# Transformer block on one core: three banks each for scores and transposed scores, products of two steps and key sums in one group

## The reference, cut to what matters

```python
x = x + attn(layernorm(x))
x = x + ffn(layernorm(x))

def attn(x):                                  # H = 8, D = 16
    q = (x @ Wq.T).reshape(b, t, 2 * H, D)    # 16 heads of queries and keys
    k = (x @ Wk.T).reshape(b, t, 2 * H, D)
    v = (x @ Wv.T).reshape(b, t, H, 2 * D)    # 8 heads of values
    q, k = rope(q), rope(k)
    probs = softmax(einsum('bhtd,bhsd->bhts', q * D ** -0.5, k))
    diff = probs[:, :, 0] - lam * probs[:, :, 1]
    attn = einsum('bhts,bhsd->bhtd', diff, v)
    attn = attn * rsqrt(mean(attn * attn, -1) + 1e-5) * (1 - LAMBDA_INIT)
    return attn.reshape(b, t, e) @ Wo.T

def ffn(x):                                   # a gated cell over the 16 sequences, in order
    c = sigmoid(x_t @ wf.T + c @ uf.T + bf) * c + sigmoid(..wi, ui, bi) * tanh(..wc, uc, bc)
    return tanh(x @ wo.T + c_final @ uo.T + bo)
```

## Time and profile before

| | |
|---|---|
| median of 3 runs | 5261.81 us (5261.59 to 5262.73) |
| profiled execution | 5259.74 us, its span 5257.9 us |
| TensorE busy (PE) | 4979.5 us, 95% |
| VectorE (DVE) | 4021.4 us, 76% |
| GpSimd (POOL) | 2891.7 us, 55% |
| ScalarE (ACT) | 2722.8 us, 52% |

### The profile page before, as it was taken

One profiled execution on the slowest core, in us unless ns is written; L12 is line 12 of the kernel. 1 busy time (PEld: TensorE's weight loads), 2 busy tenths in 40 slices (PEclk: granted clock), 3 DMA queues, 4 the chain that ended last, 5 costly groups with the idle time before them and its releaser, 6 DMA issues.

```text
span 5257.9 us, 65030 instructions
## 1 busy us (share of the span) xinstructions
PE 4979.5 (95%) x24784; PEld 1695.8 (32%) x24784; DVE 4021.4 (76%) x6183; ACT 2722.8 (52%) x3173; POOL 2891.7 (55%) x2118
## 2 busy tenths in 40 slices
PE   6999999999999999999999999999999999999999
PEld 2224232332423223242332423233242322323237
DVE  6877777877778877777887777787777887777526
ACT  1464645556465554545556454554546555463652
POOL 3573746647275573727657374664727557372750
PEclk7899999999999999999999999999999999999999
DMA  6031221302222131222303122130222213122117
GB/s 141 26 60 46 50 64 37 69 37 58 52 45 69 33 64 40 45 66 51 67 26 62 45 45 69 34 72 37 54 56 45 69 33 61 43 45 59 65 49 280
DMA packets 127706, 311.05 MB, mean 59 GB/s; under 512 B 27297, under 2 KB 30498, under 8 KB 113442
## 3 DMA queue, kind: packets, MB, share of 16 engines
q1 hardware_dynamic: 124178, 289.33, 23.2%
q10 hardware_dynamic: 3216, 17.57, 0.9%
HBM read 172.07 MB, written 99.61 MB: 52 GB/s over the span
## 4 chain that ended last, share of the span: by engine, by line
PE 64%; DVE 16%; issue 13%; POOL 3%; ACT 3%; DMA 0%; ACTq 0%; POOLq 0%; SPq 0%; DVEq 0%
PE o_ps L792 15%; PE s_ps L749 15%; PE st L777 13%; PE sum_ps L807 8%; DVE neg_max L1043 7%; PE st L891 3%; PE st L735 3%; POOL pair_sum L472 2%; PE st L717 2%; PE st L957 2%; ACT probs L564 2%; DVE stats L983 2%; DVE xa L1026 1%; DVE swapped L1021 1%; PE st L870 1%
## 5 line engine op out<-in xcount | busy, mean ns | idle before, releaser
L472 POOL TENSOR_TENSOR pair_sum<-probs 128x512 f32<-128x512 f32 x2048 | 2795.4, 1398 | 1436.4 <-ACT probs L564 1432.2
L1043 DVE TENSOR_REDUCE neg_max<-s_ps 128x1 f32<-128x512 f32 x4096 | 2679.4, 687 | 817.4 <-PE s_ps L749 810.1
L564 ACT ACTIVATE probs<-st 128x1024 f32<-128x1024 f32 x2048 | 1983.6, 1022 | 1240.9 <-PE st L777 996.0
L749 PE MATMUL s_ps<-k_stack,q_stack 96*128 96x512 bf16 x4096 | 1525.8, 393 | 140.9 <-DVE neg_max L1043 122.7
L777 PE MATMUL st<-q_stack,k_stack 99*128 99x512 bf16 x4096 | 1226.9, 385 | 20.2 <-ACT xa L512 6.6
L792 PE MATMUL o_ps<-probs,values 128*32 128x512 f32 x8192 | 1103.6, 611 | 0.7 <-ACT probs L564 0.7
L749 PEld LDWEIGHTS s_ps<-k_stack,q_stack 96*128 96x128 bf16 x4096 | 371.1, 97 | 1524.3 <-DVE neg_max L1043 1260.6
L777 PEld LDWEIGHTS st<-q_stack,k_stack 99*128 99x128 bf16 x4096 | 348.3, 99 | 792.6 <-ACT probs L564 414.8
L807 PE MATMUL sum_ps<-pair_sum,ones 128*32 128x512 f32 x4096 | 543.4, 602 | 7.7 <-POOL pair_sum L472 5.7
L891 PE MATMUL st<-xt,weights 128*128 128x512 f32 x768 | 381.7, 594 | 11.8 <-ACT xt L521 11.8
L891 PE MATMUL st<-cell_t,weights 128*128 128x512 f32 x768 | 362.9, 592 | 0.0
(11 more groups left out here) (129 smaller groups left out, 2980.3 us busy)
## 6 DMA issues: line engine op xcount, KB each, us to landing
q_stack<-qk_parts SPq DMA_DIRECT2D x384, 128.0 KB, 4.3
k_stack<-qk_parts SPq DMA_DIRECT2D x378, 128.0 KB, 7.0
swapped<-xa SPq DMA_DIRECT2D x128, 256.0 KB, 2.4
qk_parts<-swapped SPq DMA_DIRECT2D x64, 512.0 KB, 2.8
xa<-in_x SPq DMA_DIRECT2D x16, 1024.0 KB, 6.1
qk_parts<-low_part SPq DMA_DIRECT2D x64, 256.0 KB, 3.0
probs<-in_x SPq DMA_DIRECT2D x16, 1024.0 KB, 10.2
x_rows<-probs SPq DMA_DIRECT2D x16, 1024.0 KB, 3.9
```

What stands on the lines that cost most here:

```text
L472: pool.tensor_tensor(pair_sum[q % 2][:, h, :], probs[a % 4][:, h, :], probs[(a + 1) % 4][:, h, :], ALU.add)\
L564: act.activation(probs[kk % 4][:, 2 * hp:2 * hp + 2, :], st[hp][:, :, :], ACT.Exp).then_inc(exp_done, 1)
L749: pe.matmul(s_ps[i % 2][:, :], q_stack[g][0:SROWS, s, t * P:(t + 1) * P], k_stack[g][0:SROWS, s, h * HALF:(h + 1) * HALF], start=True, sto ...
L1043: dve.tensor_reduce(neg_max2[:, at, i % 2:i % 2 + 1], s_ps[i % 2][:, :], AX.X, ALU.max, negate=True).then_inc(max_done, 1)
```

## The change

- `st` becomes three banks of one tile and `s_ps` three banks of one tile (`BANKS = 3`). The ring has three slots, and `turn(i)` waits for slot `i - 3`.
- `key_tile` makes one tile with a wait and a signal of its own; tile n of a unit waits for exponential n - 3. ScalarE takes 128x512 at a time, four a step in place of two of 128x1024. GpSimd's `pair` waits for each of the four exponentials by itself.
- `score(i)` waits for `maximum(i - 3)`.
- In even steps s from 2 on, `weighted(s - 2)`, `weighted(s - 1)` and, from 4 on, `key_sums` are issued one behind the other, between `key_tile` 2 and `key_tile` 3; in odd steps none. Scores: one behind each of the first two key tiles, in odd steps one behind the third, the others behind the fourth.
- VectorE does a step's rotation operation behind the first two maxima of the step instead of behind all.
- Before LN2's transposes three gate tiles get their cell half, not four.
- The tail takes `s_ps[2]` as its fourth bank. Counters are scaled to four tiles a step (`TILES = 128`).

```diff
@@ -45,6 +45,8 @@
 SCORES = SUBS * TT * 2
+BANKS = 3
+TILES = 4 * STEPS
...
@@ -161,16 +167,18 @@
-        st = [ctx.enter_context(nc.psum_tensor(f"st{i}", [P, 2, HALF], F32)) for i in range(2)]
-        s_ps = [ctx.enter_context(nc.psum_tensor(f"s_ps{i}", [P, HALF], F32)) for i in range(2)]
+        st = [ctx.enter_context(nc.psum_tensor(f"st{i}", [P, HALF], F32)) for i in range(BANKS)]
+        s_ps = [ctx.enter_context(nc.psum_tensor(f"s_ps{i}", [P, HALF], F32)) for i in range(BANKS)]
         o_ps = ctx.enter_context(nc.psum_tensor("o_ps", [P, HALF], F32))
-        def ring(i):
-            return st[(i % 4) // 2][:, i % 2, :]
+        def ring(n):
+            return st[n % BANKS][:, :]
+
+        tail_ps = [ring(ring_base(NB - 1, True) + GEE + j) for j in range(3)] + [s_ps[2][:, :]]
...
@@ -293,7 +298,7 @@
-                attended = value(64 * (u - 1) - 16 * (1 - sub))
+                attended = value(TILES * (u - 1) - 32 * (1 - sub))
                 if not (isinstance(u, int) and u < 2):
...
@@ -463,12 +468,12 @@
-                pool.wait_ge(exp_done, 64 * u + 4 * q + 4)
                 if u > 0 or q > 1:
                 for h in range(4):
+                    pool.wait_ge(exp_done, TILES * u + 8 * q + 4 + (h + 1))
                     pool.tensor_tensor(pair_sum[q % 2][:, h, :], probs[a % 4][:, h, :],
...
@@ -509,7 +514,7 @@
                 act.wait_ge(ring_ready, rb + i + 1)
-                act.activation(dst, ring(i), func, **kw).then_inc(act_out, 1)
+                act.activation(dst, ring(rb + i), func, **kw).then_inc(act_out, 1)
...
@@ -559,9 +564,10 @@
                         act.wait_ge(pair_added, 64 * u + 4 * (kk // 2 - 1))
-                    for hp in range(2):
-                        act.wait_ge(st_ready, 64 * u + (2 * kk + hp + 1))
-                        act.activation(probs[kk % 4][:, 2 * hp:2 * hp + 2, :], st[hp][:, :, :],
+                    for h in range(4):
+                        n = 4 * kk + h
+                        act.wait_ge(st_ready, TILES * u + n + 1)
+                        act.activation(probs[kk % 4][:, h, :], st[n % BANKS][:, :],
                                        ACT.Exp).then_inc(exp_done, 1)
...
@@ -685,11 +691,14 @@
-                p = i - 4
+                p = i - BANKS
                 if WO <= p < WO + 4:
                     pe.wait_ge(act_out, ab + (act_index(p) + 1))
+
+            def bank(i, b, ab):
+                return ring(ab + (PER_ITER - ACT_ITER) * b + i)
...
@@ -744,9 +753,9 @@
                     stacked(u, 1)
-                if i >= 2:
-                    pe.wait_ge(max_done, SCORES * u + (i - 1))
-                pe.matmul(s_ps[i % 2][:, :], q_stack[g][0:SROWS, s, t * P:(t + 1) * P],
+                if i >= BANKS:
+                    pe.wait_ge(max_done, SCORES * u + (i - BANKS + 1))
+                pe.matmul(s_ps[i % BANKS][:, :], q_stack[g][0:SROWS, s, t * P:(t + 1) * P],
                           k_stack[g][0:SROWS, s, h * HALF:(h + 1) * HALF],
...
@@ -766,24 +775,21 @@
-            def key_tile(u, g, kk, hp):
+            def key_tile(u, g, kk, h):
                 th, sub, kt = kk // 16, kk // 8 % 2, kk % 8
-                if kk >= 1:
-
-                    pe.wait_ge(exp_done, 64 * u + (2 * kk + hp - 1))
-                for j in range(2):
-                    s = 2 * (2 * hp + j) + sub
-                    mm = pe.matmul(st[hp][:, j, :],
-                                   k_stack[g][0:KROWS, s, kt * P:(kt + 1) * P],
-                                   q_stack[g][0:KROWS, s, th * HALF:(th + 1) * HALF],
-                                   start=True, stop=True)
-                mm.then_inc(st_ready, 1)
+                n, s = 4 * kk + h, 2 * h + sub
+                if n >= BANKS:
+
+                    pe.wait_ge(exp_done, TILES * u + (n - BANKS + 1))
+                pe.matmul(st[n % BANKS][:, :], k_stack[g][0:KROWS, s, kt * P:(kt + 1) * P],
+                          q_stack[g][0:KROWS, s, th * HALF:(th + 1) * HALF],
+                          start=True, stop=True).then_inc(st_ready, 1)
                 r, kt = kk // 8, kk % 8
-                pe.wait_ge(exp_done, 64 * u + (2 * kk + 2))
+                pe.wait_ge(exp_done, TILES * u + 4 * (kk + 1))
                 if kt == 0 and (g == 1 or r > 0):
...
@@ -814,20 +820,23 @@
                     todo = list(plan[s])
-                    key_tile(u, g, s, 0)
-                    for i in todo[0:1]:
-                        score(un, 1 - g, i)
-                    key_tile(u, g, s, 1)
-                    for i in todo[1:2]:
-                        score(un, 1 - g, i)
-                    if s >= 1:
+                    for h in range(2):
+                        key_tile(u, g, s, h)
+                        for i in todo[h:h + 1]:
+                            score(un, 1 - g, i)
+                    key_tile(u, g, s, 2)
+                    if s >= 2 and s % 2 == 0:
+                        weighted(u, g, s - 2)
                         weighted(u, g, s - 1)
-                    for i in todo[2:4]:
-                        score(un, 1 - g, i)
                     if s >= 4 and s % 2 == 0:
                         key_sums(u, g, (s - 4) // 2)
-                    for i in todo[4:]:
+                    if s % 2 == 1:
+                        for i in todo[2:3]:
+                            score(un, 1 - g, i)
+                    key_tile(u, g, s, 3)
+                    for i in todo[2 + s % 2:]:
                         score(un, 1 - g, i)
+                weighted(u, g, STEPS - 2)
                 weighted(u, g, STEPS - 1)
...
@@ -903,14 +912,14 @@
                 pe.wait_ge(cell_ready, 4 * b + 1)
-                for i in range(4):
+                for i in range(BANKS):
                     turn(GATE + i, b, ab)
                 pe.wait_ge(xt_out, 4 * (2 * b + (2 if last else 3)))
-                for i in range(4):
+                for i in range(BANKS):
                     gate_part(i, False, False, True).then_inc(ring_ready, 1)
-                for i in range(4, 12):
+                for i in range(BANKS, 12):
                     if i == 5 and not last:
...
@@ -1040,7 +1049,7 @@
                 at = SUB_ORDER[i // 16] * TT + i % 16 // 2
-                dve.tensor_reduce(neg_max2[:, at, i % 2:i % 2 + 1], s_ps[i % 2][:, :], AX.X,
+                dve.tensor_reduce(neg_max2[:, at, i % 2:i % 2 + 1], s_ps[i % BANKS][:, :], AX.X,
                                   ALU.max, negate=True).then_inc(max_done, 1)
...
@@ -1121,11 +1130,13 @@
                         combine(u, g, s // 8 - 1)
+                    for i in itertools.islice(todo, 2):
+                        maximum(un, i)
+                    if turned is not None and s in ROPE_AT[g]:
+
+                        rope(turned, [ROPE_AT[g][s]])
                     for i in todo:
                         maximum(un, i)
-                    if turned is not None and s in ROPE_AT[g]:
-
-                        rope(turned, [ROPE_AT[g][s]])
```

More of the change, by code:

```diff
@@ L94, with ring_base @@
 NO_PLAN = [range(0)] * STEPS
+def ring_base(b, last):
+    return b * PER_ITER + (PRE - (PRE if last else 0))
 def build(nc, x, wq, wk, wv, wo_attn, lq1, lk1, lq2, lk2, wf, uf, bf, wi, ui, bi, wc, uc, bc,
@@ L236, in build @@
         block = ctx.enter_context(nc.Block())
-        def ring_base(b, last):
-            return b * PER_ITER + (PRE - (PRE if last else 0))
         def act_base(b, last):
@@ L339, in iteration @@
                     sp.wait_ge(x2_out, 16 * NB)
-                    sp.wait_ge(st_ready, 64 * (u + 1))
+                    sp.wait_ge(st_ready, TILES * (u + 1))
                     for s in range(4):
@@ L356, in iteration @@
                 if last:
-                    sp.wait_ge(st_ready, 64 * (u + 2))
+                    sp.wait_ge(st_ready, TILES * (u + 2))
                     for s in range(4, SLOTS):
@@ L716, in qk @@
                         for c in range(KC):
-                            mm = pe.matmul(ring(i), weights[:, W_Q + X, c, g * P:(g + 1) * P],
+                            mm = pe.matmul(bank(i, b, ab), weights[:, W_Q + X, c, g * P:(g + 1) * P],
                                            xt[:, c, h * HALF:(h + 1) * HALF],
@@ L731, in rows_out @@
                     for t in range(2):
-                        dst = ring(i)[:, t * E:(t + 1) * E]
+                        dst = bank(i, b, ab)[:, t * E:(t + 1) * E]
                         at = (2 * j + t) * P
@@ L869, in mean_square @@
                     turn(squares_at[i], b, ab)
-                    pe.matmul(ring(squares_at[i]), head_ones[:, :], square[:, i, :], start=True,
+                    pe.matmul(bank(squares_at[i], b, ab), head_ones[:, :], square[:, i, :], start=True,
                               stop=True).then_inc(ring_ready, 1)
@@ L890, in gate_part @@
                     for c in range(KC):
-                        mm = pe.matmul(ring(GATE + i),
+                        mm = pe.matmul(bank(GATE + i, b, ab),
```

(14 more changed lines are left out.)

## The result

The changed kernel takes 5363.6 us (5362.8 to 5376.71, four runs) against 5261.7: the ratio is 1.0201, with a 95% interval of 1.0188 to 1.0213. It is slower by 102 us. Forecast were 5390 us and slower. The profiled execution took 5363.16 us, 103.4 more than the one before.

The account below looks back on a forecast made before the run. TensorE sets the pace; grouping starves VectorE and ScalarE. Terms of +39 (g = 0 units), +40 (g = 1), +17 (last unit) and +33 (LN2) make +129 on 5259.74, about 5390 us; forecast 5310 to 5460, wider range 5225 to 5500.

Parts of the forecast that it names:

- The bound and the saving: Attention units: TensorE sets the pace; grouping three blocks takes 2.76 us and saves 0.42 us per two steps.
- The starving: Behind each group VectorE and ScalarE lack tiles: 7.07 us per two steps with eight scores against 6.77 before.
- ScalarE's idle time in a group with eight scores: Inside such a group ScalarE was to stand idle about 1 us.
- both bounds: Gap between groups: VectorE's maxima set 4.31 us with eight scores, ScalarE's exponentials 3.81 or 3.59 with five.
- Rival 1: The group pays if ScalarE and VectorE keep up: about 5105 us, or near 5200; chance 0.17.
- Rival 2: Costlier chains: products behind products at 1.09 us (+100) or exponentials at 0.60 us (+125): 5490 to 5515; chance 0.13.
- the units with g = 1: 15 attention units: 109.8 us each against 107.16, +2.65, together +40 us.
- LN2: Before LN2's transposes: one gate half moves behind them, TensorE idles some 2.7 us; +2.1 us each, x16 = +33.
- The start: Stretch up to the first unit: a change of 0 was forecast.
- Rotation at nothing: VectorE's rotation behind two maxima: put at no cost, its 1.2 to 2.3 us falling under the group in even steps.

Follow-up runs that it names:

- experiment 7: Changed kernel with each maximum and, from the second unit on, each exponential handling half the columns, the other half of that work left out: 5054.73 us.
- experiment 1: Changed kernel with the grouping alone undone, blocks issued one by one; banks, half-size exponentials and ring kept: 5265.45 us, ratio 1.001.
- experiment 3: Changed kernel with products of two steps as a group and key sums apart, one step later: 5269.58 us, ratio 1.0016.
- experiment 8: Changed kernel with the rotation operation back behind all maxima of its step: 5473.26 us.
- experiment 10: Changed kernel with a four-slot ring outside the attention, the third score bank as fourth slot, groups untouched: 5391.51 us, ratio 1.0247.
- Experiment 2: Changed kernel with four banks for transposed scores and two for scores, groups kept: 5546.39 us, ratio 1.0548.
- experiment 4: Changed kernel with the scores laid out flatter, mostly 3 in even and 4 in odd steps: 5405.53 us, ratio 1.0276.
- experiment 6: Changed kernel with each exponential, from the second unit on, handling 256 of 512 columns, that half of the work left out: 5303.13 us.
- experiment 11: Changed kernel with one extra matmul (0.86 us) in the projection between the two units of each iteration, 15 in all: 5413.59 us, ratio 1.0289.

## Why the prediction was right

**The bound and the saving** were right. The group lasts 2.72 us (2.76 forecast), and products behind products cost 0.87; I had taken 0.88 from key sums behind products.

**The starving** was right in place and size: 7.03 to 7.04 us for two steps with eight scores (7.07 forecast), a gap of 3.82 with five (3.81), 6.07 in the last unit (6.19), 108.01 for a unit (108.1). One gap of this unit was clearly missed: the one at step 20 takes 4.73 us and not 4.31. ScalarE's idle time in a group with eight scores was put too low, 2.44 us for about 1: such a gap is VectorE's, so ScalarE has emptied its banks before the group begins. The time did not hang on that. Halving each consumer by itself shows that both bounds are real and that each holds for the gaps it was worked out for; halving both shows that the group pays when nobody starves. Rival 1 is thus refuted and its condition met only in experiment 7. Rival 2's two terms did not occur (0.87 us and not 1.09, exponentials 0.49 us apart). For the units with g = 1 the agreement, +44 for +40, is in part luck. The start of such a unit took the 7.1 us forecast where the clock stayed up (7.08), and 8.95 in the four units with long falls, which the forecast did not have. And in the kernel before every one of these units has a fall; that it would stay away in ten of fifteen was not foreseen either.

**LN2** was the term that was mis-sized. The wait of 2.53 us came, but a typical iteration grew by 1.06 us and not by 2.1: the transposes came 0.66 us sooner (I allowed 0.44), and the fall of the clock that I had charged at half did not come in 13 of 15 iterations. In experiments 1, 3 and 8 it came in most of them (stretches of 92.8 to 94.5 us), though the wait was left as it is, so the wait alone doesn't decide. In experiment 10, which undid LN2's part, the whole moved the other way with the clock, but the stretches without a fall were 1.06 us shorter, the 16 us as expected.

**The start** was left out. The first unit's 128 scores have no attention beside them and run mostly at the lower clock (granted 0.59 and 0.60 from 60 to 110 us). While the clock is high, two banks are enough for a maximum every 0.60 us. When it has fallen and a score takes 0.61 us instead of 0.39, two banks let VectorE have two maxima in 1.39 us, and three let scores follow without a pause, one in 0.60. Timeline of the kernel before, at the high and at the low clock, then of the changed one, at both:

```profile
68.57 0.39 PE L749 MATMUL s_ps<-k_stack,q_stack 96*128 96x512 bf16 x1 [0.21 <-DVE neg_max L1043]
69.17 0.39 PE L749 MATMUL s_ps<-k_stack,q_stack 96*128 96x512 bf16 x1 [0.21 <-DVE neg_max L1043]
...
72.55 1.21 PE L749 MATMUL s_ps<-k_stack,q_stack 96*128 96x512 bf16 x2 [0.18 <-DVE neg_max L1043]
73.95 1.21 PE L749 MATMUL s_ps<-k_stack,q_stack 96*128 96x512 bf16 x2 [0.19 <-DVE neg_max L1043]
```

```profile
69.18 0.39 PE L758 MATMUL s_ps<-k_stack,q_stack 96*128 96x512 bf16 x1 [0.21 <-DVE neg_max L1052]
69.77 0.39 PE L758 MATMUL s_ps<-k_stack,q_stack 96*128 96x512 bf16 x1 [0.21 <-DVE neg_max L1052]
70.37 16.15 PE L758 MATMUL s_ps<-k_stack,q_stack 96*128 96x512 bf16 x27 [0.21 <-DVE neg_max L1052]
```

0.1 us for each of some hundred scores is the 10.5 us. Experiment 2, which has two score banks again, loses it again: 181.2 us up to its first unit. LN2 was forecast 18 us too high and the start 10.5; the units, 3 us longer than forecast, take back a little, and together this is the 26 us by which the sum was too high.

**Rotation at nothing** holds in so far as the units came out as forecast with it. But the edit is worth something: undone in experiment 8, it costs some 33 us at an equal clock. That fits the prediction's own remark that a score would wait without the cover of the group; the expectation of experiment 8, that the place of the operation doesn't matter, was wrong.

**What stays open:** which moment makes the clock fall after such a wait. The runs show that it comes and goes from one iteration to the next of the same kernel, and that 0.86 us more work in each iteration changes how often; they don't show the rule.

## What to carry to other kernels

Grouping work to save switches lengthens the pause of every engine that lives on the other work. Compare the group's length with what those engines really hold at its start, which is less than their banks when they are faster than the producer, and follow the gap behind the group tile by tile: latency of the first, then one consumer step per bank. And add up all that an engine has to do over several gaps: experiments 4 and 6 missed where VectorE's rotation and turning of sums were left out. In an in-order queue a tile that lacks a bank also holds back the tiles of the other consumer. And when two versions differ by less than a per cent or two, compare them stage by stage with the granted clock beside each stage, before the difference is put down to the edit.

## What the runs showed of the hardware

TensorE's granted clock fell to its lower level after waits of 2.1 to 2.7 us in some executions of a stretch and not in others with the same instructions. At the start of a unit with g = 1 the kernel before waits 2.67 us, and the clock falls in 15 of 15 such units; the changed kernel waits 2.11 us, and it falls in 5 of 15. LN2's wait of 2.53 us was followed by a fall in 2 of 15 iterations. Some 30 us into the same units TensorE waits 1.52 us in all fifteen; the clock fell there in 4, each of them a unit in which it had fallen before. Over the thirteen kernels of this study (before, after and eleven experiments), low-clock time ran from 87 to 184 us. It differed by 40 us in experiment 11, whose edit is 13 us of work. Part of this belongs to the kernel and would not average out over repeated runs: the medians of experiment 11 and the changed kernel are 50 us apart, their single runs at most 14. Another part varies between runs of one kernel. Three runs of the changed kernel had a mean clock of 0.982 and took 5362.8 to 5364.0 us, the fourth 0.978 and 5376.71; two runs of experiment 1 at 0.978 took 5258 us, three at 0.974 took 5270 to 5272.

The Trainium skill (TensorE: Matmul & The Clock Gate, Part 1: The HAM clock gate) says that the observation behind the clock is free-running and does not start with the kernel, so that the moment of a change varies from run to run. That fits these runs: the same wait of 2.11 us was followed by a clock of 1.00 and of 0.72, and between runs of one kernel the mean clock varied (0.982 and 0.978). That the moment is what decides is an inference; no run moved the moment alone.
